# Twelve groups' expert input turned by transposing transfers of 16-bit halves instead of by TensorE

## The reference

```python
gate_scores = softmax(einsum('bsd,ed->bse', x, Wg) + bg)
topk_scores, topk_idx = top_k(gate_scores, 2)
expert_outputs = einsum('bsd,eod->bseo', x, W) + b
output = sum(take_along_axis(expert_outputs, topk_idx) * topk_scores)
```

## Time and profile before

| What | Value |
| --- | --- |
| median of three runs | 511.09 us |
| the profiled execution, as timed | 510.05 us |
| its span, first to last instruction | 508.2 us |
| PE, DVE, ACT, POOL busy | 476.8, 420.2, 346.4, 348.8 us |
| TensorE clock granted, mean | 0.985 of full |

### The profile page before, as it was taken

How to read it: one execution, slowest core, us unless ns; L and a number is a source line. 1 busy time by engine, 2 the same in 40 slices (tenths; PEclk the granted TensorE clock), 3 DMA queues, 4 the chain that set the end, 5 groups by cost and what they waited for, 6 DMA issues and landing times.

```text
span 508.2 us, 14078 instructions
## 1 busy us (share of the span) xinstructions
PE 476.8 (94%) x5028; PEld 295.3 (58%) x5028; DVE 420.2 (83%) x1400; ACT 346.4 (68%) x746; POOL 348.8 (69%) x595
## 2 busy tenths in 40 slices
PE   2777989999999999999999999999999999999986
PEld 2665466556656565656656564666656565555553
DVE  6696878797987889888997889798987877788797
ACT  2466888888795866967786866968675766654312
POOL 6376235796868588785878588786858486565763
PEclk9986999999999999999999999999999999999999
DMA  6393021213221321322131422303121200110001
GB/s 203 90 258 107 28 81 36 73 57 93 58 69 28 96 74 50 79 57 72 53 94 50 77 61 69 73 25 77 33 67 30 50 4 24 21 22 22 1 23 42
DMA packets 30206, 32.12 MB, mean 63 GB/s; under 512 B 18776, under 2 KB 21048, under 8 KB 30136
## 3 DMA queue, kind: packets, MB, share of 16 engines
q1 hardware_dynamic: 29688, 30.74, 22.8%
q10 hardware_dynamic: 448, 0.48, 0.3%
HBM read 23.02 MB, written 4.47 MB: 54 GB/s over the span
## 4 chain that ended last, share of the span: by engine, by line
PE 74%; DVE 8%; ACT 4%; issue 3%; POOL 1%; DMA 1%; DVEq 0%; POOLq 0%; ACTq 0%
PE ps L2493 19%; PE ps L2557 18%; PE ps L2504 5%; PE ps L2449 5%; PE ps L2486 5%; PE ps L2427 4%; PE ps L2368 4%; PE ps L2395 3%; PE ps L2524 3%; PE ps L2525 2%; PE ps L2457 2%; ACT xn L1818 1%; PE ps L2388 1%; DVE st L1130 1%; DVE xo L1326 1%
## 5 line engine op out<-in xcount | busy, mean ns | idle before, releaser
L2557 PE MATMUL ps<-w_T,y4T 128*128 128x512 f32 x256 | 124.2, 610 | 0.7 <-DVE weighed L1308 0.7
L797 POOL TENSOR_TENSOR sum<-weighed 128x512 f32<-128x512 f32 x59 | 75.7, 1283 | 70.6 <-DVE weighed L1308 70.6
L2493 PE MATMUL ps<-h,w 128*128 128x512 f16 x512 | 120.4, 379 | 0.1
L1907 ACT ACTIVATE h<-ps 128x512 f16<-128x512 f32 x128 | 73.7, 592 | 45.2 <-PE ps L2493 35.0
L1230 DVE SCALAR_TENSOR_TENSOR h<-ps,h 128x512 f16<-128x512 f32 x128 | 85.5, 683 | 19.6 <-ACT h L1907 18.8
L1308 DVE TENSOR_TENSOR weighed<-ps,wgt 128x1024 f32<-128x1024 f32 x59 | 71.7, 1216 | 26.3 <-PE ps L2557 25.8
L2493 PEld LDWEIGHTS ps<-h,w 128*128 128x128 f16 x512 | 48.2, 98 | 55.8 <-issue 6.6
L1869 ACT ACTIVATE prT<-ps,maskT 77x1024 f32<-77x1024 f32 x64 | 67.4, 1103 | 14.6 <-PE ps L2427 11.5
L762 POOL TENSOR_TENSOR rs<-ve,neg_half 128x4 f32<-128x4 f32 x64 | 65.9, 1030 | 8.7
L2557 PEld LDWEIGHTS ps<-w_T,y4T 128*128 128x128 f32 x256 | 44.4, 189 | 42.4 <-issue 38.6
L1165 DVE TENSOR_REDUCE mx<-ps 128x8 f32<-128x616 f32 x64 | 47.8, 788 | 10.2 <-PE ps L2395 10.2
(11 more groups left out here) (170 smaller groups left out, 910.4 us busy)
## 6 DMA issues: line engine op xcount, KB each, us to landing
cx<-in_ctx SPq DMA_DIRECT2D x16, 320.0 KB, 3.6
vx<-in_values SPq DMA_DIRECT2D x16, 320.0 KB, 3.2
kT<-in_keys SPq DMA_DIRECT2D x16, 308.0 KB, 2.9
xa<-in_x SPq DMA_DIRECT2D x16, 256.0 KB, 2.7
out_x<-xo SPq DMA_DIRECT2D x16, 256.0 KB, 2.1
plugs<-plug_d SPq DMA_DIRECT2D x16, 77.0 KB
w_T<-in_weights SPq DMA_DIRECT2D x1, 592.0 KB, 4.3
weighed<-in_weights SPq DMA_DIRECT2D x1, 592.0 KB, 6.0
```

The lines of the kernel that those rows point to most:

```text
L797: nc.gpsimd.tensor_tensor(sum4[:], both[:, 0:4 * D], both[:, 4 * D:8 * D], ALU.add).then_inc(c_sum4.sem, 1)
L1907: last = nc.scalar.activation(h[:, 0, (k - 1) % FC, :], src, ACT.Relu)
L2493: last = pe.matmul(pb(g, k), w2[:, i, c * 128:(c + 1) * 128], h1[:, g.p, part, i, :], start=(i == 0 and part == 0), stop=(i == FC - 1 and ...
L2557: last = pe.matmul(pm(g, j)[:, half, :], y4T[:, g.p, j * S:(j + 1) * S], w_moeT[:, half * 512:(half + 1) * 512], start=True, stop=True)
```

## The change

For groups 2 to 13 (`parted(g)`, twelve groups) the turn of block d leaves PE. Groups 0, 1, 14 and 15 keep it. A new ACT instruction `d_halves` reads each fp32 number of `xn` as two 16-bit integers and writes the low and the high halves apart into `zp`. A new transposing transfer `d_move` on SP turns `zp` into `zq`. `d_turned` then reads `zq` instead of PSUM and joins the halves in `y4T`. `zp` and `zq` have one buffer each: `d_move` waits for the join of the group before, `d_halves` for the transfer of the group before.

All five written-out lists are in another order as well. Two tables of the setup now stand in `xo`, which is not yet in use then, to make room.

```diff
+        zp = sb("zp", [128, 2, W], U16)
+        zq = sb("zq", [128, 2, W], U16)
...
+        def parted(g):
+
+            return TD <= g.n < NG - 2
...
+            def d_move(g):
+
+                sp.wait_ge(d_split.sem, d_split.of(d_at(g)))
+                if g.has(TD + 1):
+                    sp.wait_ge(d_yT.sem, d_yT.of(g, back=1))
+                sp.dma_start_transpose(zq[:].rearrange("c half (j s) -> c (half j) s", j=G),
+                                       zp[:].rearrange("s half c -> s (half c)")).then_inc(d_moved.sem, 16)
...
             def d_turned(g):
-                act.wait_ge(d_turn.sem, d_turn.of(g))
+                if parted(g):
+                    act.wait_ge(d_moved.sem, d_moved.of(d_at(g)))
+                else:
+                    act.wait_ge(d_turn.sem, d_turned_by_pe(g))
...
+                if parted(g):
+                    nc.scalar.activation(y4T[0:D - 1, g.p].bitcast(U16).rearrange("c (s h) -> c h s", h=2),
+                                         zq[0:D - 1], ACT.Copy).then_inc(d_yT.sem, 1)
+                    return
                 nc.scalar.activation(y4T[0:D - 1, g.p], pt(g)[0:D - 1, :], ACT.Copy).then_inc(d_yT.sem, 1)
...
+            def d_halves(g):
+
+                act.wait_ge(ln_d.xn.sem, ln_d.xn.of(g))
+                if g.has(TD + 1):
+                    act.wait_ge(d_moved.sem, d_moved.of(d_at(g), back=1))
+                nc.scalar.activation(zp[:], xn[3][:, g.p, :].bitcast(U16).rearrange("s (c h) -> s h c", h=2), ACT.Copy
+                                     ).then_inc(d_split.sem, 1)
...
             e_experts(g[9], 3, (c_x3, g[10]))
-            b_layer(g[11], 6)
-            d_turns(g[10], (c_weighed, g[9], 4))
+            a_scores(g[14], 1, (a_max[0], g[14]))
             b_layer(g[11], 7)
```

More of the change, by code:

```diff
@@ L619, in _ @@
             load_context(g[11])
+            d_move(g[4])
+            plug(g[8])
             store(g[3])
@@ L626, in _ @@
             spread_maxima(g[8])
+            load_context(g[12])
             plug(g[9])
-            load_context(g[12])
+            d_move(g[5])
+            b_turn(g[7])
             store(g[4])
-            b_turn(g[7])
             load_keys(g[10])
@@ L634, in _ @@
             spread_maxima(g[9])
+            load_context(g[13])
+            d_move(g[6])
             plug(g[10])
-            load_context(g[13])
+            b_turn(g[8])
             store(g[5])
-            b_turn(g[8])
             load_keys(g[11])
@@ L644, in _ @@
             load_context(g[14])
-            store(g[6])
+            d_move(g[7])
             b_turn(g[9])
             load_keys(g[12])
+            store(g[6])
             load_values(g[12])
@@ L659, in _ @@
             plug(g[13])
-            store(g[8])
+            d_move(g[9])
             b_turn(g[11])
             load_keys(g[14])
+            store(g[8])
             load_values(g[14])
@@ L674, in _ @@
             spread_maxima(g[15])
+            d_move(g[12])
+            b_turn(g[14])
             store(g[11])
-            b_turn(g[14])
             b_turn(g[15])
+            d_move(g[13])
             store(g[12])
@@ L2808, in _ @@
-            a_scores(g[11], 1, (a_max[0], g[11]))
-            b_layer(g[8], 8)
+            b_layer(g[8], 6)
+            a_scores(g[11], 1, (a_max[0], g[11]))
+            b_layer(g[8], 7)
+            b_layer(g[8], 8)
+            a_weights(g[10], 0, (a_max[1], g[11]))
+            e_experts(g[6], 3, (c_x3, g[7]))
+            b_last(g[8])
+            d_gate_scores(g[7], (c_weighed, g[6], 4))
             d_gate_turn(g[7])
-            a_weights(g[10], 0, (a_max[1], g[11]))
+            a_weights(g[10], 1, (a_prT[0], g[10]))
```

973 lines of the change are left out of this document (494 added, 479 removed).

## The result

The changed kernel took 524.74 us (median of three runs, 523.72 to 527.41) against 511.09, a ratio of 1.0264 with a 95% interval from 1.0232 to 1.0296. Forecast were 506.7 us, with a range up to 513.5.

The account below looks back on a forecast made before the run. PE was taken as the bound, busy 395.7 of 400 us in the middle. Terms -5.3 - 2.5 - 0.9 + 2.1 + 2.2 = -4.4 us took 511.09 to 506.7 us, range 500.5 to 513.5 for 8 in 10.

Parts of the forecast that it names:

- PE's start-to-start price: Twelve groups' four transposes leave PE, costed at 0.44 us a group from start to start: 5.3 us gained.
- The fourth rival: On PE, a transpose costs its mean duration of 289 ns, so 48 give 13.9 us: 498.1 us, chance 0.03.
- Each microsecond that PE's queue really loses in the middle is gained, as long as nobody is late for it: PE, busy 395.7 of 400 us from 80 to 480 us, was taken as the bound, so its losses count in full.
- the first two terms: On PE, 5.3 us for the transposes removed and 2.5 us for waits directly ahead of them, both gained.
- The 2.5 us of waits ahead of the turns: PE's step excesses over 1.73 us ahead of the twelve turns, released by `xn` and the banks' last read, counted as gained.
- The new order of the other calls ... I also cost at nothing, with 1.5 us either way: Reordering the other calls, and the setup, costs nothing, with 1.5 us either way in the range.
- ACT ... has room on average: ACT gains 18 us of work from split and join, reaching about 308 of 392 us in the middle.
- The chain: Projection to gate scores through `xn`, split, transfer and join takes 11.5 us; groups 6, 8 and 11 short, 2.1 us lost.
- The list of distances: PE work between projection and gate scores in groups 2 to 13: 10.8 to 13.8 us, 10.8 in groups 6, 8, 11.
- The third rival: Gate scores wait for `y4T` on a longer chain: 523.5 us with slow split and join, 520.2 with late landings; chance 0.12.
- Gate turns behind the scores: In groups 3, 7, 9, 10 and 14 PE waits 0.45 us for the scores' copy: 2.2 us lost.
- SP: Twelve more transfers of 1.26 us each to issue, in an otherwise mostly waiting queue, costed at nothing.

Follow-up runs that it names:

- late gate scores: Changed kernel with the join reading with a step, and PE's gate scores and gate turns of groups 4, 6, 8 and 11 one call later: 539.36 us.
- early gate scores: New order without transfer, split and join cut to 16 numbers from group 3 on, gate scores of eight groups earlier on all queues: 526.61 us.

## Why the prediction was wrong, step by step

- **PE's start-to-start price**: right. 5.3 forecast, 5.5 measured by doubling. The fourth rival (13.9) is refuted. (The 275 ns that it quotes stand on that page for a transpose of bf16 numbers; those here are of fp32 numbers.)
- **"Each microsecond that PE's queue really loses in the middle is gained, as long as nobody is late for it"**: this base of the sum failed. Removing the turns in the old order gives 1.6 us where the first two terms had 7.8. The 2.5 us of waits ahead of the turns were the sign: their releasers `xn` and `weighed` said that PE was already early there. I counted those waits as a gain, and I looked for slack at the gate scores in group 10 alone, which has 0.96 us of it where five other groups have next to none.
- **"The new order of the other calls ... I also cost at nothing, with 1.5 us either way"**: the largest miss. It costs 9 us at equal work, about 18 with the turns in it where the run put them. The prediction looked at the places where calls of block d moved, and only there. That the order costs this much is shown; by what path it does is not.
- **"ACT ... has room on average"**: true as an average and no argument. In the old order each microsecond of 9.4 to 22 us of ACT work cost 0.46 to 0.64 us, for the split mostly through the chain to the gate scores. In the new one split and join are worth 3.3 us, part of it their length in the chain.
- **The chain**: split 1.06 and landing 3.1 right, join 1.35 instead of 1.05; the chain was 12.0 to 12.7 us to most groups' gate scores instead of 11.5. The sum added up the pieces and left out that the join waits in ACT's list behind a read of PSUM that itself waits for PE. The list of distances was right in most groups: with the way left out the gate scores come 10.6 us behind the projection in groups 6, 8 and 11, where it had 10.8. The third rival had the place right, and the gate scores did wait 8.9 instead of 2.1 us; its causes, 2.1 us for each of split and join or 4.8 us for every landing, did not occur (the longest join took 1.36 us, the median landing 3.1). And taking the whole way out gives back 6.3 us, not half of the result. That its times (520.2 and 523.5) are near the measured one is luck: a price too large there, and nothing elsewhere.
- **Gate turns behind the scores**: 2.2 forecast, 2.0 counted, and no gain to be had: moved away, the kernel is slower.
- **SP**: the twelve transfers are worth 3 us. Their length reaches the gate scores in part of the groups only; nothing in the runs points to their issue.

In one line: before 511.1; turns off PE, -1.6; the new order, +8.8; split and join, +3.3; the transfer, +3.0; together 524.6. These are the steps between kernels in one order, so they add up to the measured 524.7 by construction, and each is good to about 2 us; in another order they would be others, as the 18 us of the new order with turns show.

The Trainium skill, page "SBUF — State Buffer", section "SBUF: two separate sides", has a step within a line of 16 bytes for free. The split agrees (a step of 4 bytes in its input, 1.057 us). The join with a step of 4 bytes in its output took 1.350 us, and 1.172 with the step in its input instead, where successive numbers lie 1 KB apart; so for a 16-bit output of ACT the measurement differs from the rule.

No version in these runs beats the kernel before but the one that leaves out the turns, by 0.3%. A turn of any kind that took no time would bring little more in the old order, some 3 us by the estimate above.

## What to carry to other kernels

Before costing a removal from the busiest queue at its full size, ask in every group what arrives just in time for it: even waits of 0.2 us ahead of the removed calls mean that the queue is already early there, and that something else is the bound. This kernel, whose queues are all written out and meet at semaphores, is balanced on several chains at once: added work cost on both queues that were tried (0.5 to 1 us for each microsecond), and removed work paid little. In a chain of pieces count what stands ahead of each piece in its own queue, and not the lengths alone. Where a variant makes PE wait for some microseconds at a time, read the granted clock before the waits are blamed for all of the loss. If a change rewrites the order, the order is the change: price it first, by a run of the new order with the old work.

## What the runs showed of the hardware

- A stepped 16-bit write by ACT of 127 x 1024 numbers took 1.350 us, the same join with a stepped read 1.172, and the stepped read of the split (128 x 1024) 1.057.
- Eight transposes in a row cost PE twice what four do: a turn written twice pushed the next layer from 0.46 us to 0.90 us after its start (369.73 and 370.63 in that trace).
- The transposing transfer of 256 KB took 3.1 us to landing in the median, 4.8 at most, like those of block b (3.1 and 4.7). Its issue on SP took 1.23 to 2.09 us.
- Around waits of PE of 2.4 us (late gate scores, groups 6, 8 and 11), 4.2 us (early gate scores, group 2) and 3.1 to 6.1 us (old order with the new way, all twelve groups) the granted clock stood at 1.2 GHz for 3.4 or 6.8 us. An expert took 3.57 us from start to start in such a stretch, and 1.82 at 2.4 GHz. In the changed kernel the clock stayed at 2.4 GHz in the middle.
